# Spectral operator block: last modes ahead of the first output, waits on the real matmuls, the last batch's second part earlier, nine matmuls ahead of the first load

## What is computed

```python
xa   = gn(x).reshape(B*C, 1, H, W);  xa_n = inorm(xa)
k, q = spec_conv(xa_n, kw), spec_conv(xa_n, qw)     # 8x8 modes, to 64x64
v    = spec_conv(xa_n, vw)                          # 8x8 modes, to 256x256
att  = softmax(q @ k.T * sqrt(64*64)) @ v           # 64 x 64 images
att  = inorm(att) + xa;  att_n = inorm(att)
mix  = spec_conv(att_n, mix_w) + mix_bias           # 32x32 modes
skip = att_n * skip_w + skip_b
out  = inorm(inorm(mix + skip)) + att
return x + out.reshape(x.shape)
```

## Time and profile before

| | us |
|---|---|
| median of 3 runs | 711.17 (709.3 to 713.19) |
| the profiled execution, its own time | 708.26 |
| its span, on which all stretches below are counted | 706.2 |
| forward stage of batch 0, from the start | about 72 |
| attend and produce of batches 0, 1, 2 | about 172, 170, 169 |
| attend and produce of batch 3 | about 124 |

### The profile page before, as it was taken

The page is one execution under the profiler, slowest core; times in us unless marked ns, Lnnn a source line. Parts: engine busy times, 40 slices in busy tenths (PEclk is TensorE's granted clock), DMA queues, the critical chain, the costliest instruction groups (busy, mean ns, idle before and its releaser), DMA issues.

```text
span 706.2 us, 15104 instructions
## 1 busy us (share of the span) xinstructions
PE 659.0 (93%) x5772; PEld 589.9 (84%) x5772; DVE 485.6 (69%) x1099; ACT 334.8 (47%) x722; POOL 356.8 (51%) x430
## 2 busy tenths in 40 slices
PE   6999998999999998999999989899999999988796
PEld 6999898788888898878888889878888888986574
DVE  3566566678767676577777765867777766656787
ACT  5888041464666513255566633236466660424141
POOL 1700024968980003795993002398699000359995
PEclk9999899999999999999999999999999999999799
DMA  8990000799889500199788910059979970005567
GB/s 265 389 361 3 1 1 2 226 309 296 284 302 301 192 1 1 52 317 328 259 307 289 304 56 1 1 174 316 316 263 304 296 242 1 1 1 209 205 245 297
DMA packets 71687, 136.32 MB, mean 193 GB/s; under 512 B 5376, under 2 KB 5888, under 8 KB 71616
## 3 DMA queue, kind: packets, MB, share of 16 engines
q1 hardware_dynamic: 71616, 135.36, 56.3%
HBM read 68.23 MB, written 67.11 MB: 192 GB/s over the span
## 4 chain that ended last, share of the span: by engine, by line
PE 63%; DVE 14%; POOL 13%; DMA 3%; issue 3%; ACT 2%; SPq 1%; DVEq 0%; ACTq 0%; POOLq 0%
PE psY L306 27%; PE psP L361 13%; POOL X L744 9%; PE psP L417 4%; PE psY L327 4%; PE psT L343 4%; PE psP L327 3%; DVE X L796 3%; DVE Y L796 3%; DVE SQ L796 2%; DMA X<-in_x 2%; DMA out<-X 1%; DVE QP L832 1%; ACT SQ L515 1%; POOL ALPHA L737 1%
## 5 line engine op out<-in xcount | busy, mean ns | idle before, releaser
L744 POOL TENSOR_TENSOR X<-X,ALPHA 128x512 f32<-128x512 f32 x244 | 254.8, 1082 | 27.5 <-DVE IM L1032 25.5
L306 PE MATMUL psY<-FWD,X 128*128 128x128 f32 x2048 | 248.3, 280 | 6.8 <-DMA X<-in_x 6.8
L306 PEld LDWEIGHTS psY<-FWD,X 128*128 128x128 f32 x2048 | 236.7, 194 | 21.5 <-issue 19.1
L796 DVE TENSOR_TENSOR X<-X,psP 128x512 f32<-128x512 f32 x240 | 155.7, 684 | 73.6 <-PE psP L361 60.9
L832 DVE TENSOR_REDUCE QP<-SQ 128x32 f32<-128x512 f32 x256 | 161.8, 679 | 63.4 <-ACT SQ L515 42.2
L361 PE MATMUL psP<-INVW,T 64*128 64x256 f32 x960 | 147.4, 406 | 19.5 <-DVE X L796 16.1
L515 ACT ACTIVATE SQ<-X 128x512 f32<-128x512 f32 x256 | 147.1, 622 | 16.0 <-DVE Y L803 9.1
L722 POOL TENSOR_TENSOR Y<-Y,OMEGA 128x256 f32<-128x256 f32 x32 | 25.3, 790 | 249.6 <-ACT Y L519 249.3
L361 PEld LDWEIGHTS psP<-INVW,T 64*128 64x128 f32 x960 | 94.9, 190 | 51.3 <-issue 39.4
L537 ACT ACTIVATE T<-psT,BIA,SCL 128x256 f32<-128x256 f32 x128 | 65.3, 561 | 116.3 <-PE psT L343 105.3
L507 ACT ACTIVATE Y<-psY 128x512 f32<-128x512 f32 x128 | 76.0, 594 | 66.2 <-PE psY L306 65.6
(11 more groups left out here) (189 smaller groups left out, 463.3 us busy)
## 6 DMA issues: line engine op xcount, KB each, us to landing
X<-in_x SPq DMA_DIRECT2D x128, 512.0 KB, 5.2
out<-X SPq DMA_DIRECT2D x128, 512.0 KB, 4.1
INVH<-t_inv_h SPq DMA_DIRECT2D x1, 256.0 KB, 4.9
LW<-in_low_w SPq DMA_DIRECT2D x1, 204.0 KB, 3.4
GWT<-t_w SPq DMA_DIRECT2D x1, 192.0 KB, 4.9
FWD<-t_fwd SPq DMA_DIRECT2D x1, 128.0 KB, 2.2
INVW<-t_inv_w SPq DMA_DIRECT2D x1, 128.0 KB, 4.7
LM<-in_low_mix SPq DMA_DIRECT2D x1, 68.0 KB, 3.0
```

Of the source, the lines that this page charges most:

```text
L306: last = mm(psY[p % 2][:, (2 * i + c) * 128:(2 * i + c + 1) * 128], X[:, 2 * p + i, a, c * 128:(c + 1) * 128], FWD[:, a, :], start=a == 0, ...
L744: P.tensor_tensor(v, v, al, MUL).then_inc(x_scaled, 1)
L796: return V.tensor_tensor(out, a, b, op)
```

## The change

Five things.

1. `modes(b, 11)` goes ahead of `energy(b, 0)`, so two of the last four calls stand between energy and spread as before, but they are now 12 and 13; 14 stands ahead of `inverse_h(b, 0)`, and 15, which was done behind the first quad of outputs, ahead of the first output. ACT's `mode_powers` and DVE's `weigh_modes` for that last group move from u = 1 to u = 0. POOL's place for the last group is unchanged for batches 0 to 2 (ahead of image 8).
2. The six `wait_alone` are gone; the semaphore is waited for by the real matmul behind it.
3. In the last batch the second part's steps move from u = 3, 4, 6, 7, 8 to u = 1, 2, 4, 5, 6 (`second(b)`) on all engines; POOL weighs the last group ahead of image 3 (was 6), DVE folds it at u = 1 (was 2).
4. POOL's wait for the second part's coefficients (ahead of image 24, in the last batch 20) stays for batches 0 to 2 and is gone in the last.
5. Ahead of the first load PE does nine 128x128 matmuls on the ones, waiting only for the first DVE memset.

```diff
+        def second(b):
+            return LAG if b < B - 1 else 1
...
-            def wait_alone(semaphore, count, ps=psA):
-                pe.wait_ge(semaphore, count)
-                mm(ps[:, 0:1], ONES[0:64, :], ONES[0:64, 0:1], start=True, stop=True)
...
                 j0, j1 = (0, 4 * SPLIT) if part == 0 else (4 * SPLIT, 32)
-                wait_alone(d_made, 2 * b + part + 1, psB)
+                pe.wait_ge(d_made, 2 * b + part + 1)
...
-                wait_alone(qk_ready, b + 1)
+                pe.wait_ge(qk_ready, b + 1)
...
-                for q in range(6, 2 * SPLIT + 1):
+                for q in range(6, 2 * SPLIT + 2):
                     modes(b, q)
                 energy(b, 0)
-                modes(b, 2 * SPLIT + 1)
                 modes(b, 2 * SPLIT + 2)
+                modes(b, 2 * SPLIT + 3)
                 spread(b, 0)
                 turn_low(b, 0)
-                modes(b, 2 * SPLIT + 3)
+                modes(b, 2 * SPLIT + 4)
                 inverse_h(b, 0)
-                modes(b, 2 * SPLIT + 4)
+                modes(b, 2 * SPLIT + 5)
...
-                    if u == LAG:
+                    if u == second(b):
                         energy(b, 1)
-                    if u == LAG + 1:
+                    if u == second(b) + 1:
                         pe.wait_ge(var_made, 2 * b + 2)
-                    if u == LAG + 3:
+                    if u == second(b) + 3:
                         spread(b, 1)
-                    if u == LAG + 4:
+                    if u == second(b) + 4:
                         pe.wait_ge(c2_kept, 2 * b + 2)
                         turn_low(b, 1)
...
-                    if u == 0:
-                        modes(b, 2 * SPLIT + 5)
...
+            pe.wait_ge(setup_vec, 1)
+            for n in range(9):
+                mm(psZ[0][:, 0:128], ONES[:, :], ONES[:, :], start=True, stop=True)
             pe.wait_ge(fwd_in, 16)
...
-                behind = {2: SPLIT + 1, 8 if b < B - 1 else 6: SPLIT + 2}
+                behind = {2: SPLIT + 1, 8 if b < B - 1 else 3: SPLIT + 2}
...
-                        if i == 4 * LAG + (12 if b < B - 1 else 8):
+                        if i == 4 * LAG + 12 and b < B - 1:
                             pool.wait_ge(coef_made, 2 * b + 2)
...
-                    if u == 1:
+                    if u == 0:
                         weigh_modes(b, SPLIT + 2)
-                    if u == 2:
+                    if u == (2 if more else 1):
                         fold_powers(b, SPLIT + 2)
                         halve_energies(b, 1)
```

More of the change, by code:

```diff
@@ L429, in attend @@
                 modes(b, 2)
-                wait_alone(qk_kept, 2 * b + 2)
+                pe.wait_ge(qk_kept, 2 * b + 2)
                 for n in range(4):
@@ L436, in attend @@
                 modes(b, 4)
-                wait_alone(probs_made, b + 1)
+                pe.wait_ge(probs_made, b + 1)
                 nc.tensor.transpose(psB[0:IMGS, 320:384], PR[:, 0, :], EYE[:, :]).then_inc(probs_turned, 1)
                 modes(b, 5)
-                wait_alone(probs_kept, b + 1)
+                pe.wait_ge(probs_kept, b + 1)
                 mm(psA[0:IMGS, 0:2 * LOW], PR[:, 1, :], QKV[:, 2, :, :].rearrange("p r n -> p (r n)"),
                    start=True, stop=True).then_inc(att_made, 1)
-                for q in range(6, 2 * SPLIT + 1):
+                for q in range(6, 2 * SPLIT + 2):
                     modes(b, q)
                 energy(b, 0)
-                modes(b, 2 * SPLIT + 1)
                 modes(b, 2 * SPLIT + 2)
+                modes(b, 2 * SPLIT + 3)
                 spread(b, 0)
                 turn_low(b, 0)
-                modes(b, 2 * SPLIT + 3)
+                modes(b, 2 * SPLIT + 4)
                 inverse_h(b, 0)
-                modes(b, 2 * SPLIT + 4)
+                modes(b, 2 * SPLIT + 5)
             def produce(b, more):
@@ L462, in produce @@
                         forward(b + 1, 2 * (u - LAG) + 1)
[L463 removed]
+                    if u == second(b):
                         energy(b, 1)
[L465 removed]
+                    if u == second(b) + 1:
                         pe.wait_ge(var_made, 2 * b + 2)
[L467 removed]
+                    if u == second(b) + 3:
                         spread(b, 1)
[L469 removed]
+                    if u == second(b) + 4:
                         pe.wait_ge(c2_kept, 2 * b + 2)
                         turn_low(b, 1)
[L472 removed]
+                    if u == second(b) + 5:
                         pe.wait_ge(d_added, 6 * b + 6)
@@ L608, in produce @@
                         keep_t(b, 2 * u + 1)
-                    if u == 1:
+                    if u == 0:
                         mode_powers(b, SPLIT + 2)
-                    if not more and u in (2, LAG + 5):
+                    if not more and u in (2, second(b) + 5):
                         vector_alphas(b, int(u > 2))
-                    if u in (LAG, LAG + 1):
-                        turn_group(b, SPLIT + 1 + u - LAG)
-                    if u == LAG + 4:
+                    if u in (second(b), second(b) + 1):
+                        turn_group(b, SPLIT + 1 + u - second(b))
+                    if u == second(b) + 4:
                         act.wait_ge(d_made, 2 * b + 2)
-                    if u == LAG + 5:
+                    if u == second(b) + 5:
                         low_piece(b, 2)
@@ L1086, in second_part @@
             def second_part(b, u, more):
-                if u == LAG:
+                if u == second(b):
                     deviations(b, 1)
-                if u == LAG + (2 if more else 1):
+                if u == second(b) + (2 if more else 1):
                     coefficients(b, 1)
-                if u == LAG + 3:
+                if u == second(b) + 3:
                     keep_spread(b, 1)
                     low_outputs(b)
-                if u == LAG + 4:
+                if u == second(b) + 4:
                     add_low(b, 2)
```

1 line of the change is left out of this document (removed).

## The result

The changed kernel takes **699.19 us** (median of 4 runs, 698.85 to 701.88), against 711.08 for the kernel before on the same chip (4 runs, 709.3 to 713.19): a ratio of 0.984, with an interval of 0.9804 to 0.9876. Two later sets, on other occasions, gave 698.0 (ratio 0.9825) and 698.87 (0.9854). The forecast was 701.0. Ratios and intervals leave out a run that lies over 1.5% above the fastest of its kernel; of all runs named here that is one, the 708.81 us of e_waits.

A forecast was written before the change was run, and what follows sets the result against it. PE bounds most stretches, DVE steps and POOL the others. Batches gain 2.9 + 1.5 + 1.5 + 2.6, the last stretch 3.2, less 1.4 at the start: 10.3 off 708.26, plus 2.9 for the median: 701.0 us, range 696.5 to 706.

The forecast's parts named there:

- What bounds the kernel: PE bounds most stretches, small DVE steps the one before energy, POOL that from spread; POOL's first scaling at 120.7 us.
- Part 1, dummies: In attend, four waiting matmul pairs leave PE's chain: 1.2 us a batch; the sixth gives 0.3 in batches 0 to 2.
- Part 2, energy and idle: At energy, modes 11 fills PE's 1.96 us idle: energy 1.15 us earlier, and 1.4 us of clock in two of four batches.
- Part 3, last batch: From POOL's start to DVE's end, the moved second part and dropped wait give 70.4 us against 73.6: 3.2 us less.
- the one on POOL beside DVE: In the last batch, coefficients and low outputs beside scaling cost POOL's limit 0.5 to 1.5 us, of which 0.5 is free.
- Part 4, head: At the start, nine matmuls gain nothing; PE's idle grows from 0.39 to 2.1 us and half clock behind it costs 1.4.
- The sum: Over the whole kernel: gains of 11.7 us less 1.4 at the start, so 10.3 us, giving 701.0 us.
- The sign that was to refute it: In the forward stages: the prediction is wrong altogether if they get longer or the clock falls inside them.
- That of 699 us: No clock fall at the start and POOL's limit reached in the last batch: 1.9 us better, chance 0.17.
- That of 704: The last batch gives nothing, as early energy keeps PE waiting and DVE never gets even: 3.2 us lost, chance 0.14.
- That of 707: In attend and turn_low the dummies were filler and waits replace them: 4.8 and 0.9 us lost, chance 0.08.
- The slower one: Gaps under POOL give half clock, 3 x 3.4 us, and start and last batch 2 each: 715 us, chance 0.06.

The follow-up runs named there:

- e_waits: The kernel before with only the six dummy matmuls taken out, the real matmul carrying the wait: 702.16 us, ratio 0.988.
- e_modes: The kernel before with only the order of the last five calls of modes changed, dummies and last batch as they were: 706.6 us, ratio 0.9954.
- e_head: The kernel before with only the nine matmuls ahead of the first load added: 708.88 us, ratio 0.9993.
- e_loads: The changed kernel with the first six image loads ahead of the 15 table loads and the waits for the tables moved back: 695.73 us, ratio 0.9798.
- after: The changed kernel in its first set, median 699.19 us; its profiled execution, which gives the trace, took 701.88 us.
- before: The kernel without the change, median 711.08 us beside the changed kernel; its profiled execution, which gives the trace, took 708.26 us.
- after_again: The changed kernel, nothing varied, measured and profiled a second time: 698.0 us, ratio 0.9825.
- e_fill: The changed kernel with eight more idle matmuls between the fourth and the fifth forward: 700.31 us, ratio 0.9861.
- e_nohead: The changed kernel without the nine matmuls at the start: 697.09 us, ratio 0.9821.
- f_after: The changed kernel, nothing varied, in a later set beside a version without the last batch's move: 698.87 us, ratio 0.9854.

## Why the prediction was right, and where it was not

The time, the direction and the size are right: 701.0 forecast, 699.19 measured, inside the range. By its steps:

- **What bounds the kernel.** Right. The stretch from spread to the first forward is POOL's and has the same 19.5 us in all traces, and POOL's first scaling came at 120.95 us (120.7 predicted).
- **Part 1, dummies: 1.2 us a batch.** Right, and slightly too much: 1.06 to 1.07. Why 0.1 us came back is not shown. The estimate of 0.85 us for the four, worked out from the Trainium skill ("TensorE: Matmul & The Clock Gate", "LDWEIGHTS (loading the stationary operand)"), is too low; the rows were the better source. The 0.3 us at the sixth dummy can't be seen, since the forward stages differ by 3.8 us between executions.
- **Part 2, energy and idle.** Energy 1.15 us earlier: 1.07. The idle gone: 0.17. The 1.15 us is booked under the modes there, but it is all due to the dummies, as its own term for DVE's chain (1.2 us earlier) implies: e_modes alone starts energy no earlier, and what the moved modes give is the clock. The clock, 1.4 us in two of four batches, is 1.63 in about two of four on average; a single execution may have it in all four, as e_head did. Modes 15 ahead of the first output cost nothing, as said.
- **Part 3, last batch: 3.2 us.** The stretch is right (70.1 against 70.4; over seven traces 70.6) and its shares are wrong. A third of it comes from the modes, and the moved second part brings 0.7 us in the medians. The step that failed is the one on POOL beside DVE. It looked for 0.5 to 1.5 us on POOL, which has none (POOL's own way is 67.8 us, 69.9 less the two waits is 67.9), and let DVE's steps keep their durations; there the price was 2.8 us. By the Trainium skill ("GPSIMD Engine Reference", "1. Specifications") the engines share SBUF interfaces; the traces agree, with DVE steps that end 0.03 to 0.05 us behind POOL's instruction. The moved energy was said to cost nothing, though the clock might fall: PE's idle there was 3.49 us (2.7 estimated), the clock fell behind it every time, and the stage is up to 1.3 us longer where it stayed low longest.
- **Part 4, head: +1.4 us.** Wrong as a typical value. It came true in the profiled execution (+1.5 us, the idle of 2.08 us and the clock of 0.51 just as described), but in one trace of six; the medians show nothing. An idle there was taken as sure to bring the lower clock where the rows already had one without it. What was right is that the gain is nothing because the fifth load doesn't move, and e_loads shows it from the other side.
- **The sum.** From the traces: 4.3 for the dummies, 3.3 for the clock, 2.9 for the last batch (of seven traces), head 0, so 10.5 us; the three sets of medians give 11.5 to 11.9. What is left, about 1 us, has no row (the sixth dummy may be in it). The forecast's own terms add up to 11.5 before rounding, not 11.7. The forecast's 10.3 came out near in part because two errors met: a loss of 1.4 us at the head that seldom comes, and gains summed to 11.7 where these terms give 10.5. That part is luck.
- **The sign that was to refute it.** "Wrong altogether if the forward stages get longer": they are 107.4 us in the mean in after against 106.8 in before, and 106.4 in after_again. They vary by more than that within one kernel, so one trace can't be read for this sign. The clock fell inside one stage of e_fill: the last 16 passes ahead of attend of batch 3 took 3.13 us behind an idle of 1.87 us, and 2.07 us in after.

**The rivals.** That of 699 us named no fall at the start, which is right, and POOL's limit reached, which happens in some executions only (after, e_nohead and e_fill, with 70.1). That of 704, nothing from the last batch, is refuted for the stretch and half true for the moved part. That of 707, the dummies as filler, is refuted by e_waits: energy does come 1.06 us earlier. The slower one is refuted under POOL by the rows at 127.81 to 136.34: gaps, and no half clock. Its half clock in the last batch did come, and its 2 us at the start in one trace of six (1.5 us).

## What to carry to other kernels

An idle of PE of some 2 us can cost nearly as much again behind it (1.63 us behind 1.96). Filling it cured the clock with useful work and with empty work alike; the empty work cost 0.17 us a time. A wait is sometimes a shield: before taking one from an engine, look at what its neighbour does in that time on the same memory. And one trace is one draw: with transfers on the path, compare the terms that repeat and leave sums to the medians of runs.

## What the runs showed of the hardware

- A half clock behind an idle came 9 of 12 times behind 1.96 us at energy, 1 of 6 times behind 1.4 to 2.8 us at the start, and 14 of 14 times behind the two idles of 3.2 to 3.9 us in the last batch; how long it lasted there differed between executions of one kernel (7 us in all in after, 14 in f_after).
- A waiting matmul of one column costs 0.27 us of the path on average (1.07 for four), though its row on the chain says 0.31.
- DVE steps of 32 to 64 columns on 64 partitions, from SBUF to SBUF, took up to five times as long beside POOL: 1.84 against 0.37 us for two, 1.12 against 0.24 for one. Each ended 0.03 to 0.05 us behind POOL's instruction (28 of 28), so what it cost was the rest of that instruction. DVE's 128x512 steps with an input in PSUM kept their 0.69 us beside it.
- A store and a load behind it, each of two images, took 8.2 to 10.6 us at the ends of the batches, and the last store 3.2 to 4.6 us, in the same kernel and without any edit near.
- At the very start PE runs at half speed while the granted clock reads 1.00: in before the first four forwards took 10.32 us for 64 passes, and in after, behind the nine matmuls, 8.1 for the same. The 1.00 is a lack of records there: in all 14 traces the first clock record begins within 0.3 us of PE's first quick pass (at 11.36 us in before, at 5.84 in after).
